# Turning h by 32x32 squares on VectorE and 32 DMAs a batch instead of on TensorE, from batch 2 on

## The reference, cut to what matters

```python
def _ln(x, g, b):
    m = jnp.mean(x, axis=-1, keepdims=True)
    v = jnp.mean((x - m) ** 2, axis=-1, keepdims=True)
    return (x - m) * jax.lax.rsqrt(v + EPS) * g + b

h = _ln(x, pw_g[pathway_ids], pw_b[pathway_ids])      # 500 rows to gather from
h = _ln(h, cp_g[compartment_ids], cp_b[compartment_ids])   # 5 rows
t = _ln(x, tm_g[time_steps], tm_b[time_steps])
s = _ln(x, ms_g[scale_type], ms_b[scale_type])
m, n, r = (x + _mlp_ln(state, ...)[:, None, :] for each of 3 states)
w = softmax(aw)
cat = concatenate([w[0]*h, w[1]*t, w[2]*m, w[3]*n, w[4]*r, w[5]*s], axis=-1)   # 3072 features
out = x + _ln(silu(cat @ int_W1 + int_b1) @ int_W2 + int_b2, int_g, int_be)
```

## Time and profile before

| | |
|---|---|
| three runs | 995.85 us median, 994.02 to 996.64 |
| the profiled execution | 994.5 us, of which the profile's span is 992.8 |
| TensorE (PE) busy | 976.8 us, 98% of the span |
| VectorE (DVE) busy | 800.0 us, 81% |
| GpSimd (POOL) busy | 505.4 us, 51% |
| ScalarE (ACT) busy | 272.1 us, 27% |
| granted TensorE clock, mean | 0.995 |
| DMA | 141.7 MB, mean 143 GB/s |

### The profile page before, as it was taken

The page is one execution under the profiler, slowest core; times in us unless marked ns, Lnnn a source line. Parts: engine busy times, 40 slices in busy tenths (PEclk is TensorE's granted clock), DMA queues, the critical chain, the costliest instruction groups (busy, mean ns, idle before and its releaser), DMA issues.

```text
span 992.8 us, 13724 instructions
## 1 busy us (share of the span) xinstructions
PE 976.8 (98%) x4436; PEld 802.4 (81%) x4436; DVE 800.0 (81%) x1102; ACT 272.1 (27%) x341; POOL 505.4 (51%) x624
## 2 busy tenths in 40 slices
PE   7999999999999999999999999999999999999997
PEld 6677887888888888888888888888888888888885
DVE  6986988697887979878797887879788787987855
ACT  4633232231232322132222312323122232313311
POOL 3442556375554746555374544637445474655322
PEclk9999999999999999999999999999999999999999
DMA  9953546444364553535545363554436355353122
GB/s 317 332 199 117 198 100 191 128 125 143 92 198 98 162 155 82 192 85 179 127 158 139 76 208 85 172 145 127 144 89 206 90 162 153 89 188 86 42 64 64
DMA packets 52738, 141.70 MB, mean 143 GB/s; under 512 B 10200, under 2 KB 10456, under 8 KB 48752
## 3 DMA queue, kind: packets, MB, share of 16 engines
q0 software_dynamic: 22976, 66.07, 26.4%
q1 hardware_dynamic: 29744, 75.41, 21.7%
HBM read 124.55 MB, written 16.90 MB: 142 GB/s over the span
## 4 chain that ended last, share of the span: by engine, by line
PE 84%; DVE 2%; issue 0%; POOL 0%; POOLq 0%; DVEq 0%
PE hid_ps L1327 20%; PE hid_ps L1326 20%; PE hid_ps L1325 20%; PE o_ps L1432 5%; PE o_ps L1431 5%; PE o_ps L1430 5%; PE made_ps L1305 3%; PE made_ps L1318 2%; PE hid_ps L1330 1%; DVE xc L805 0%; PE made_ps L1446 0%; DVE r_sb L943 0%; PE made_ps L1447 0%; PE made_ps L1448 0%; DVE yst L881 0%; DVE fst L927 0%
## 5 line engine op out<-in xcount | busy, mean ns | idle before, releaser
L1325 PE MATMUL hid_ps<-cat_hi,w_hi 128*128 128x512 f32 x1008 | 395.8, 393 | 0.0
L1327 PE MATMUL hid_ps<-cat_hi,w_lo 128*128 128x512 f32 x1008 | 392.9, 390 | 0.0
L1326 PE MATMUL hid_ps<-cat_lo,w_hi 128*128 128x512 f32 x1008 | 392.9, 390 | 0.0
L1325 PEld LDWEIGHTS hid_ps<-cat_hi,w_hi 128*128 128x128 f32 x1008 | 189.7, 188 | 40.1 <-issue 1.7
L1327 PEld LDWEIGHTS hid_ps<-cat_hi,w_lo 128*128 128x128 f32 x1008 | 189.5, 188 | 39.6
L1326 PEld LDWEIGHTS hid_ps<-cat_lo,w_hi 128*128 128x128 f32 x1008 | 189.6, 188 | 38.4
L490 POOL DMA_INDIRECT pw_rows<-cp,class_now x64 | 128.5, 2008 | 66.6 <-DVE y_sb L872 55.2
L659 ACT ACTIVATE cat_hi<-v_ring 128x1024 fp32r<-128x1024 f32 x64 | 68.0, 1062 | 303.3 <-DVE v_ring L854 303.2
L483 POOL DMA_INDIRECT pw_rows<-pw,path_now x64 | 98.4, 1537 | 62.1 <-DVE y_sb L890 41.5
L504 POOL DMA_DIRECT2D r_sb<-x x60 | 57.8, 964 | 109.7 <-DVE r_sb L952 99.0
L437 POOL TENSOR_TENSOR fve<-fmv,eps_col 128x1 f32<-128x1 f32 x64 | 28.5, 445 | 139.4 <-DVE fmv L909 127.1
(11 more groups left out here) (157 smaller groups left out, 1239.2 us busy)
## 6 DMA issues: line engine op xcount, KB each, us to landing
x_sb<-x SPq DMA_DIRECT2D x16, 1024.0 KB, 6.3
out<-r_sb SPq DMA_DIRECT2D x64, 256.0 KB, 2.0
xc<-xT SPq DMA_DIRECT2D x15, 1024.0 KB, 5.0
r_sb<-x POOLq DMA_DIRECT2D x60, 256.0 KB, 4.8
stats_bc<-token_stats SPq DMA_DIRECT2D x30, 256.0 KB, 5.2
ids_sb<-ids SPq DMA_DIRECT2D x16, 256.0 KB, 7.3
keep<-int_W SPq DMA_DIRECT2D x12, 256.0 KB, 7.1
w_raw<-int_W SPq DMA_DIRECT2D x12, 256.0 KB, 10.6
```

The lines of the kernel that those rows point to most:

```text
L1325: pe.matmul(acc, w1_hi[:, k, cols], hi, start=start, stop=False)
L1326: pe.matmul(acc, w1_hi[:, k, cols], lo, start=False, stop=False)
L1327: return pe.matmul(acc, w1_lo[:, k, cols], hi, start=False, stop=stop)
```

## The change

Tokens get their natural order in the batch (token 128 g + 32 t + i stands on partition 32 g + i, tile t; inputs are laid out so by the host: `xp`, `xT`, `ids`, `pid`), so a statistics row is contiguous over the tokens. The statistics go through a 32x32 transposition on VectorE (`turn_stats`) and four DMAs to DRAM instead of one. From batch 2 on the normed y is written into the free half of `pw_rows` (`y_normed`), VectorE transposes it in 32x32 squares into `y_sb` (`y_turn`, four a batch), and SP issues 2 x 16 DMAs a batch (`h_move`) of 32 partitions x 2 runs of 128 floats (512 B) each, into `v_ring`, from where `h_high` and `h_low` read. TensorE's `fill_h` stays for batches 0 and 1 alone. `gather` waits for the turning, as the half of `pw_rows` holds y until then, and GpSimd's list is reordered.

```diff
+    stats_dram = nc.dram_tensor("token_stats", (4, TT, P), f32, kind="Internal").ap()
...
-        stats_bc = sb("stats_bc", [P, P, 2, TT])
+        stats_bc = sb("stats_bc", [P, 2, TOKENS])
...
+        def by_pe(b):
+            return isinstance(b, int) and b < 2
+        def y_normed(b, t):
+            return y_sb[:, t, :] if by_pe(b) else pw_rows[:, t, D:2 * D]
+        def h_from(b, i):
+            return made_ps[:, :, :] if by_pe(b) else v_ring[:, slot(H0 + i), :, :]
...
+            def h_move(b, i):
+                sp.wait_ge(y_turned, TT * (b - 1))
+                sp.nop(nofuse=True)
+                sp.wait_ge(used, 6 * b + 3 + i)
+                for g in range(P // 32):
+                    for a in range(P // 32):
+                        sp.dma_start(v_ring[32 * a:32 * a + 32, slot(H0 + i), :, g * P:(g + 1) * P],
+                                     y_sb[32 * g:32 * g + 32, 2 * i:2 * i + 2, a * P:(a + 1) * P]).then_inc(h_in[i], 16)
...
             def spread_stats(b):
-                sp.wait_ge(x_packed, 4 * b + 2)
-                sp.dma_start(stats_dram.rearrange("v p m -> p v m"),
-                             x_pack[:, :, :, :].rearrange("p v s t -> p v (s t)")).then_inc(stats_out, 16)
-                sp.wait_ge(stats_out, 16 * b)
+                sp.wait_ge(pack_turned, b)
+                for g in range(P // 32):
+                    sp.dma_start(stats_dram[:, g, :].rearrange("m (t i) -> m t i", i=32), pack_rows[32 * g:32 * g + 4 * TT, :]
+                                 ).then_inc(stats_out, 16)
+                sp.wait_ge(stats_out, 64 * b)
...
                 if not (first or last):
                     load_x(b + 1)
                     load_ids(b + 1)
+                if last:
+                    load_residual()
+                if not by_pe(b):
+                    h_move(b, 0)
+                if not (first or last):
                     load_xT(b + 1)
+                if not by_pe(b):
+                    h_move(b, 1)
                 if not first:
                     store(b - 1, 0)
...
             def gather(b, t):
-                wait(pool, yscaled, TT * (b - 1) + t + 1)
+                if by_pe(b - 1):
+                    wait(pool, yscaled, TT * (b - 1) + t + 1)
+                else:
+                    pool.wait_ge(y_turned, TT * (b - 3) + t + 1)
...
+            def chunk(b, last=False):
+                if by_pe(b):
                     path_ids(b + 1)
                     gather(b + 1, 0)
                     gather(b + 1, 1)
+                for t in (2, 3):
+                    gather_class(b, t)
+                for t in (2, 3):
+                    y_rstd(b, t)
+                if not (last or by_pe(b)):
+                    path_ids(b + 1)
+                    gather(b + 1, 0)
+                    gather(b + 1, 1)
+                out_rstd(b - 1, 0)
                 if not last:
                     gather(b + 1, 2)
                     gather(b + 1, 3)
                     class_ids(b + 1)
+                add_x(b - 1, 0)
+                out_rstd(b - 1, 1)
...
             def h_high(b, i):
-                act.wait_ge(filled, 6 * b + FT + i + 1)
+                if by_pe(b):
+                    act.wait_ge(filled, (FT + 2) * b + FT + i + 1)
+                else:
+                    act.wait_ge(h_in[i], 16 * 16 * (b - 1))
                 act.wait_ge(used, 6 * b + 3 + i)
-                act.activation(cat_hi[:, slot(H0 + i), :, :], made_ps[:, :, :], ACT.Copy).then_inc(h_hi_done, 1)
+                act.activation(cat_hi[:, slot(H0 + i), :, :], h_from(b, i), ACT.Copy).then_inc(h_hi_done, 1)
...
+            def turn_stats(b):
+                dve.wait_ge(x_packed, 4 * b + 2)
+                wait(dve, stats_out, 64 * (b - 1))
+                dve.transpose(pack_rows[:, :], pack_cols[:, :]).then_inc(pack_turned, 1)
...
-                mean = stats_bc[:, :, 0, :].rearrange("q p t -> q t p").unsqueeze(1).to_broadcast([P, FT, TT, P])
-                v = xc[:, :, :].rearrange("q f (t p) -> q f t p", t=TT)
-                dve.tensor_tensor(v, v, mean, ALU.subtract).then_inc(centred, FT)
+                mean = stats_bc[:, 0:1, :].to_broadcast([P, FT, TOKENS])
+                dve.tensor_tensor(xc[:, :, :], xc[:, :, :], mean, ALU.subtract).then_inc(centred, FT)
...
+                dve.scalar_tensor_tensor(scaled[:, :], ids_sb[:, :], cls_val[:, 0:1], stats_bc[:, 1, :],
                                          ALU.is_equal, ALU.mult).then_inc(scaled_ready, 1)
...
+            def y_turn(b, t):
+                dve.wait_ge(yscaled, TT * (b + 1))
+                dve.wait_ge(yhat_done, TT * b + t + 1)
+                dve.transpose(y_sb.rearrange("q f (a t i) -> q (f a) t i", t=TT, i=32)[:, :, t, :],
+                              y_normed(b, t).rearrange("q (a i) -> q a i", i=32)).then_inc(y_turned, 1)
...
                     y_norm(b, 2)
+                    y_norm(b, 3)
                     ts_mult(b, 2)
-                    y_norm(b, 3)
+                    y_turn(b, 0)
+                    y_turn(b, 1)
                     ts_low(b, 2)
                     out_stats(b - 1, 0, o_ps[:, 0, :])
+                    y_turn(b, 2)
+                    y_turn(b, 3)
...
                     h_low(b, 0)
+                    if not last:
+                        turn_stats(b + 1)
...
                     second(b - 1, 2)
                     pair(b, 4)
-                fill_h(b, 0)
-                half_pair(b, 5, 0)
-                fill_h(b, 1)
-                half_pair(b, 5, 1)
+                    pair(b, 5)
                 second(b - 1, 3)
```

More of the change, by code:

```diff
@@ L32, with build @@
 HI, LO, AGAIN, SCL = 0, 32, 64, 16
-def build(nc, x, xT, ids, pid, small, small_at, tm_g, ms_g, rows, net_vecs, pw, cp, W1s, W2s, int_W1, int_W2, out):
+def build(nc, x, xp, xT, ids, pid, small, small_at, tm_g, ms_g, rows, net_vecs, pw, cp, W1s, W2s, int_W1, int_W2, out):
     f32, f32r, i32 = mybir.dt.float32, mybir.dt.float32r, mybir.dt.int32
@@ L203, in build @@
         ids_in = sem("ids_in")
+        h_in = [sem(f"h_in{i}") for i in range(2)]
         stats_out = sem("stats_out")
@@ L535, in _, with first_chunk @@
                 y_rstd(0, t)
-            def chunk(b, first=False, last=False):
-                if not last:
+            def first_chunk():
+                path_ids(1)
+                gather(1, 0)
+                gather(1, 1)
+                net_rstd()
+                x_rstd(1)
+                gather(1, 2)
+                gather(1, 3)
+                class_ids(1)
+                gather_class(1, 0)
+                gather_class(1, 1)
+                y_rstd(1, 0)
+                y_rstd(1, 1)
+            def chunk(b, last=False):
+                if by_pe(b):
                     path_ids(b + 1)
@@ L553, in chunk @@
                     class_ids(b + 1)
[L554 to L558, removed]
-                    x_rstd(b + 1)
[L560 to L564, removed]
+                add_x(b - 1, 0)
+                out_rstd(b - 1, 1)
+                if not last:
+                    x_rstd(b + 1)
+                add_x(b - 1, 1)
+                out_rstd(b - 1, 2)
+                add_x(b - 1, 2)
+                out_rstd(b - 1, 3)
                 if not last:
@@ L567, in chunk @@
                     gather_class(b + 1, 1)
-                if not first:
-                    add_x(b - 1, 3)
+                add_x(b - 1, 3)
                 if not last:
@@ L572, in chunk @@
                     y_rstd(b + 1, 1)
-            chunk(0, first=True)
+            first_chunk()
             chunk(1)
@@ L1297, in fill @@
                 if j == 0:
+                    wait(pe, v_done, FT * b)
                     wait(pe, h_lo_done, 2 * b)
@@ L1317, in fill_h @@
                     for t in range(TT):
[L1318 removed]
+                        ins = pe.transpose(by_tiles(made_ps[:, half, :])[:, t, :, :], y_sb[:, t, f * P:(f + 1) * P], ident)
                 ins.then_inc(filled, 1)
```

82 lines of the change are left out of this document (45 added, 37 removed).

## The result

The changed kernel takes 1049.42 us (median of 4 runs, 1048.51 to 1053.0) against 995.28 for the kernel before, in runs beside it: a ratio of 1.056, 95% interval 1.0544 to 1.0575. It is 54 us slower, some 3.9 us for each of the 14 batches. The prediction had said 971.

A forecast was written before the change was run, and what follows sets the result against it. TensorE's list of work was taken as the bound, before and after: 994.5 less 25.2 us for the transposes gives 969.3, or 971 at the median of runs. Own range 967 to 977, chance 0.54; full range 967 to 1015.

The forecast's parts named there:

- the first rival: SP's queue becomes the bound from 0.535 us an issue; 1020 us at 0.58, 1068 at 0.67; chance 0.27.
- TensorE's transposes, 1.8 us a batch, 25 in all: TensorE's list loses 16 transposes a batch in batches 2 to 15: 1.8 us each batch, 25.2 in all.
- (e): TensorE's 2.0 us wait in batch 2 may shrink with the shorter `centre`; up to 2 us in the range.
- Turns, `centre`, `scaled_next`: VectorE a batch: four turns add 2.8 us, contiguous reads save 1.8 in `centre` and 0.47 in `scaled_next`; sum 49.0.
- The estimate of 1.24 us: One VectorE turn of 512 elements, scaled from the skill's 311 ns for 128x128; the prediction took 0.70.
- The price of an issue, p = 0.47: SP's time for each DMA issue, taken from prologue loads: 0.47 us, bounds 0.32 and 0.67.
- The loop through SP: Chain of waits each batch: SP's 38 issues 17.9 us, statistics' landing and broadcasts 7.3, VectorE 31.3; sum 56.5.
- the class row: VectorE's 0.85 us wait a batch for it should go, as GpSimd no longer issues two large gathers ahead.
- the 0.6 us of room against TensorE: The loop through SP at 56.5 us a batch just fits under TensorE's 57.1.
- Edge (a), `h_low` 1 before the last pairs: `h_low` 1 ends at 546 to 549, TensorE needs its tile at 549.8: fits by 1 to 4 us.
- The Trainium skill's 50 ns: Skill's sequencer time for one issue; would make SP's part 1.9 us instead of 17.9; rejected for the trace rows.

The follow-up runs named there:

- the run with rows 6 KB apart: Changed kernel with h's 32 issues writing to DRAM rows 6 KB apart instead of 4, `h_high` reading `y_sb` unmoved: 985.69 us, ratio 0.9917.
- the kernel with joined issues: Changed kernel with both tiles of h in one group of 16 issues a batch, four runs each, after both slots are free: 1040.14 us, ratio 1.0478.
- the kernel with runs of 2 KB: Changed kernel with 16 h issues a batch, one 2 KB run a partition, and `turn_stats` ahead of `h_low` 0: 988.53 us, ratio 0.9948.

## Why the prediction was wrong

The mechanism was named, as the first rival, with 0.27; the forecast itself failed, and 1049 lies outside the range.

- **TensorE's transposes, 1.8 us a batch, 25 in all.** Right for the loop: 1.80 measured, 57.12 us a batch without transfers against 57.1. That run is 20 us quicker than the kernel before and not 25; 2.7 us are lost by the rest of the change in the first three batches, which the prediction had put at nothing, or (e) at a gain.
- **Turns, `centre`, `scaled_next`.** Right. The groups after, against the earlier trace rows:

```profile
L968 DVE STREAM_TRANSPOSE y_sb<-pw_rows 128x512 f32<-128x512 f32 x56 | 36.2, 683 | 0.0
L878 DVE TENSOR_TENSOR xc<-xc,stats_bc 128x2048 f32<-128x2048 f32 x15 | 34.4, 2293 | 9.3 <-DMA stats_bc<-token_stats 8.1
L913 DVE SCALAR_TENSOR_TENSOR scaled<-ids_sb,small_sb,stats_bc 128x512 fp32r<-128x512 int32 x15 | 11.3, 751 | 37.7 <-issue 37.7
```

  A turn takes 0.68 (0.70 taken), `centre` 2.29 (2.3), `scaled_next` 0.75. The estimate of 1.24 us scaled from the Trainium skill ("VectorE: DVE Perf Modes", "The three transpose paths") is not what these rows show; the 0.68 decides.
- **The price of an issue, p = 0.47.** This is the step that failed. It measured 0.65, near the upper bound of 0.67, though not by a piling up of transfers: behind the end, with nothing beside it, an issue from SBUF to SBUF takes 0.63 to 0.65. "By the row nearest in kind and not the cheapest" went by partitions and runs; what counted was that those rows have one side in DRAM. The rows had two hints that I passed over: no SBUF-to-SBUF issue stood in the trace at all, and with 38 issues in the loop an error of 0.065 decided the sign. (The 36 more issues of its heading are 35: 32 for h and 3 for the statistics.) With both ends of the bound so unequal in their results, 0.54 for the forecast was too much.
- **The loop through SP.** Right in its links and order, and with p put in right it gives 24.7 + 7.3 + 31.3 = 63.3 against 63.0 measured. But that is in part luck, as two of its parts missed in opposite ways. VectorE's part is 32.2 instead of 31.3: the class row is still waited for (13.0 us in 14 batches, where 0.85 us a batch was to go). SP's issues and the landings are 30.8 instead of 32.0. The four writes are 0.65 each too, but they are part of the 38. With p at 0.47 to 0.49 for h's issues, in the run with rows 6 KB apart, issues and landings took 25.7 us (25.2 in the sum) and VectorE 32.3, together 58.0 us, so the 0.6 us of room against TensorE were not there.
- **Edge (a), `h_low` 1 before the last pairs.** It is where TensorE stands, one of the places that the first rival named. Without the slow issues it is no bound (no such wait with rows 6 KB apart).
- **The 1.7 to 3 us at the lower clock after most waits** were not in the sum. In the changed kernel they lie in time that the loop takes anyway: its links through SP and VectorE make the 63.0 us without them. In the kernel with joined issues TensorE was a link of the loop, and in the batches that had them they cost time.
- **The Trainium skill's 50 ns** for a sequencer's dispatch ("DMA: Bandwidth & Descriptors", "Anatomy of one DMA — SWDGE (gpsimd) path") is given for a DMA that GpSimd issues. The time that SP's queue spends on an issue is another, here 0.33 to 0.80 by form, and no figure of that section stands for it.

## What to carry to other kernels

Before work is moved into many small DMAs, write down the whole loop of waits through the issuing queue, count the issues in it, and get the price of that very form from a short run behind the end of the kernel: in the two runs with h's issues to DRAM, 0.64 against 0.47 to 0.49 us an issue turned 0.8% faster into 5.3% slower. What stands behind a long row of issues in the same queue (here 8 KB of statistics) pays for all of it. A detour by DRAM with few, wide transfers was quicker than 32 narrow ones from SBUF to SBUF.

## What the runs showed of the hardware

An issue of SP with one run a partition costs 0.63 us from SBUF to SBUF and 0.45 with one side in DRAM, with 32 partitions as with 128. With DRAM on one side it cost 0.64 again where two runs a row join with the rows into one dimension in DRAM but not in SBUF; 2 KB of padding a row brought 0.47 to 0.49 back, and 62 us in the kernel. Eight runs take 0.65 to 0.8. SP's and ScalarE's queues issue side by side almost undisturbed (10.9 and 11.4 us for 16 each, 10.3 for SP alone). TensorE ran at 1.2 GHz for 3.4 us soon after a wait of 3.4 us for h; after waits of 1.9 to 3.1 us it did so in some batches and not in others, and after waits of 0.4 to 0.9 us in the loop of the kernel with runs of 2 KB it did not.
